# One bin to each half of TensorE's rows: the last stage of a graph layer pair with room for 320 rows a bin

## The reference, cut to what matters

```
h     = max(layernorm(x), 0)
out   = h @ W_self.T + b_self
neigh = h[dst] @ W_neigh.T + b_neigh          # one row per edge
agg   = segment_sum(neigh, src)               # rows of one source added up
count = max(segment_sum(1, src), 1)
x     = x + out + agg / count
```

## Time and profile before

| | |
|---|---|
| three runs, median (lowest to highest) | 1936.53 us (1936.05 to 1937.86) |
| the profiled execution | 1934.63 us, of which 1932.4 us is the span from the first to the last instruction |
| TensorE busy | 1740.7 us, 90% of the span, granted clock 0.955 on average |
| VectorE, ScalarE, GpSimd busy | 1463.5, 1122.0, 1138.4 us |
| the last stage, from its first matmul to its last | 1610.8 to 1922.9 us |

### The profile page before, as it was taken

How to read it: one execution, slowest core, us unless ns; L and a number is a source line. 1 busy time by engine, 2 the same in 40 slices (tenths; PEclk the granted TensorE clock), 3 DMA queues, 4 the chain that set the end, 5 groups by cost and what they waited for, 6 DMA issues and landing times. The chain is left out here.

```text
span 1932.4 us, 46473 instructions
## 1 busy us (share of the span) xinstructions
PE 1740.7 (90%) x11686; PEld 1343.8 (70%) x11686; DVE 1463.5 (76%) x4618; ACT 1122.0 (58%) x2713; POOL 1138.4 (59%) x938
## 2 busy tenths in 40 slices
PE   2659679999999999999999999999999845888998
PEld 1223257777777777777777777777777645888897
DVE  8989547877777777777777877777877625777886
ACT  1017668877777777777777777777764312333333
POOL 6970244366666666666666666666653363556676
PEclk9769769999999999999999999999999987999999
DMA  2000045677777777777777767677767556999876
GB/s 79 0 1 1 28 112 160 204 223 240 231 225 234 228 223 237 235 223 235 228 223 235 235 205 214 212 204 212 220 195 213 156 163 193 274 279 285 250 221 177
DMA packets 342167, 372.54 MB, mean 193 GB/s; under 512 B 40508, under 2 KB 269758, under 8 KB 342078
## 3 DMA queue, kind: packets, MB, share of 16 engines
q1 hardware_dynamic: 265246, 293.99, 51.2%
q0 software_dynamic: 25088, 51.83, 8.9%
q10 hardware_dynamic: 51744, 25.70, 4.4%
HBM read 251.54 MB, written 119.82 MB: 192 GB/s over the span
## 5 line engine op out<-in xcount | busy, mean ns | idle before, releaser
L764 POOL DMA_INDIRECT xg<-in_x,srcs x392 | 435.3, 1110 | 440.8 <-issue 362.0
L775 POOL DMA_INDIRECT row_table<-row_out,posq x392 | 387.3, 988 | 194.7 <-issue 125.8
L1231 PE MATMUL psum<-bin_rows,bin_hot 128*128 128x129 f32 x2352 | 288.6, 281 | 47.9 <-DVE bin_hot L1204 47.8
L1231 PEld LDWEIGHTS psum<-bin_rows,bin_hot 128*128 128x128 f32 x2352 | 274.0, 194 | 62.6 <-issue 30.8
L1102 PEld LDWEIGHTS psum<-hwin,hotT 128*128 128x128 f32 x1568 | 186.9, 195 | 78.3 <-issue 68.8
L1004 ACT ACTIVATE nhT<-psum 128x512 f32<-128x512 f32 x98 | 58.5, 597 | 309.8 <-PE psum L1074 309.8
L887 DVE TENSOR_TENSOR hotT<-dst_keys,reach 128x1024 f32<-128x1024 int32 x98 | 120.8, 1232 | 139.5 <-PE psum L1102 138.2
L1102 PE MATMUL psum<-hwin,hotT 128*128 128x128 f32 x1568 | 204.4, 285 | 15.6 <-DMA hwin<-h_table 9.9
L1091 PE MATMUL psum<-hot,win 128*128 128x128 f32 x1568 | 191.6, 275 | 1.4 <-DVE hot L859 1.4
L1091 PEld LDWEIGHTS psum<-hot,win 128*128 128x128 f32 x1568 | 183.4, 192 | 1.6 <-DVE hot L859 1.6
L1204 DVE TENSOR_TENSOR bin_hot<-iota,bin_rel 128x1536 f32<-128x1536 f32 x98 | 174.4, 1779 | 5.3
(11 more groups left out here) (174 smaller groups left out, 3761.9 us busy)
## 6 DMA issues: line engine op xcount, KB each, us to landing
win<-msg_table SPq DMA_DIRECT2D x392, 129.0 KB
hwin<-h_table SPq DMA_DIRECT2D x392, 128.0 KB
bin_rows<-row_table SPq DMA_DIRECT2D x196, 195.0 KB, 3.2
msg_table<-msgw SPq DMA_DIRECT2D x98, 258.0 KB, 4.0
nx<-in_x_nodes SPq DMA_DIRECT2D x98, 256.0 KB, 4.1
h_table<-h1s SPq DMA_DIRECT2D x98, 256.0 KB
dst_keys<-in_dst_rows SPq DMA_DIRECT2D x98, 256.0 KB
y_table<-ys SPq DMA_DIRECT2D x61, 256.0 KB, 4.1
```

What stands on the lines that cost most here:

```text
L764: nc.gpsimd.indirect_dma_start(out=xg[:, par, t, :], out_offset=None, in_=ins["x"], in_offset=bass.IndirectOffsetOnAxis(ap=srcs[:, par, t: ...
L775: nc.gpsimd.indirect_dma_start(out=row_dram, out_offset=bass.IndirectOffsetOnAxis(ap=posq[:, par, t:t + 1], axis=0), in_=row_out[:, par, t ...
L1231: last = nc.tensor.matmul(bank[2 * slot + b][:, h * MW:(h + 1) * MW], bin_hot[:, slot % 2, b, w, h * P:(h + 1) * P], bin_rows[:, slot, b, ...
```

## The change

A bin has room for 320 rows in place of 384. Its rows are laid on 64 partitions, five rows each, and the two bins of a quad lie in the two halves of the 128 partitions: bin 0 in partitions 0 to 63, bin 1 in 64 to 127. So a load moves 64 runs of 2600 bytes in place of 128 of 1560. The one-hot matrix has 5 by 256 = 1280 columns, and both halves compare with 0 to 255; a new table `qbin`, loaded at the start, holds the first node of the bin for each half. The sums become 20 matmuls over 64 rows each, with the two bins alternating: one in the lower half of the array's rows and into one bank, the next in the upper half and into the other bank. The zero rows behind the table are written by two DMAs in place of one. The limit for the general program falls to 320 with `BCAP`.

```
-BTILES = 3
-BCAP = BTILES * P
+HALF_P = P // 2
+BT = 5
+BCAP = BT * HALF_P
...
+        qbin = sb("qbin", [P, QUADS])
-        weights += [(qbase, "qbase"), (iota4, "iota4")]
+        weights += [(qbase, "qbase"), (qbin, "qbin"), (iota4, "iota4")]
...
-                sp.dma_start(row_dram[ROWS:ROWS + BCAP, :].rearrange("(p w) c -> p (w c)", p=P), pads[:, 0:BTILES * RW]).then_inc(pads_set, 16)
+                sp.dma_start(row_dram[ROWS:ROWS + 3 * HALF_P, :].rearrange("(p w) c -> p (w c)", p=HALF_P), pads[0:HALF_P, 0:3 * RW]).then_inc(pads_set, 16)
+                sp.dma_start(row_dram[ROWS + 3 * HALF_P:ROWS + BCAP, :].rearrange("(p w) c -> p (w c)", p=HALF_P), pads[0:HALF_P, 0:2 * RW]).then_inc(pads_set, 16)
...
+                def half_at(b):
+                    return slice(HALF_P * b, HALF_P * b + HALF_P)
...
-                            sp.dma_start(bin_rows[:, slot, b, :, :].rearrange("p w c -> p (w c)"),
-                                         row_dram[bass.ds(start, BCAP), :].rearrange("(p w) c -> p (w c)", p=P)).then_inc(rows_loaded[slot], 16)
+                            sp.dma_start(bin_rows[half_at(b), slot, :, :].rearrange("p w c -> p (w c)"),
+                                         row_dram[bass.ds(start, BCAP), :].rearrange("(p w) c -> p (w c)", p=HALF_P)).then_inc(rows_loaded[slot], 16)
...
-                        nc.vector.tensor_scalar(bin_rel[:], bin_rows[:, slot, :, :, C + 1], qbase[:, bass.ds(q, 1)], None, ALU.subtract).then_inc(f_rel, 1)
+                        nc.vector.tensor_scalar(bin_rel[:], bin_rows[:, slot, :, C + 1], qbin[:, bass.ds(q, 1)], None, ALU.subtract).then_inc(f_rel, 1)
...
-                        nc.vector.tensor_tensor(bin_hot[:, par, :, :, :], iota4[:].rearrange("p (b n) -> p b n", b=2).unsqueeze(2).broadcast_to([P, 2, BTILES, BIN]),
-                                                bin_rel[:].unsqueeze(3).broadcast_to([P, 2, BTILES, BIN]), ALU.is_equal).then_inc(f_hot, 1)
+                        nc.vector.tensor_tensor(bin_hot[:, par, :, :], iota4[:, 0:BIN].unsqueeze(1).broadcast_to([P, BT, BIN]),
+                                                bin_rel[:].unsqueeze(2).broadcast_to([P, BT, BIN]), ALU.is_equal).then_inc(f_hot, 1)
...
-                        for b in range(2):
-                            for h in range(2):
-                                for w in range(BTILES):
-                                    last = nc.tensor.matmul(bank[2 * slot + b][:, h * MW:(h + 1) * MW], bin_hot[:, slot % 2, b, w, h * P:(h + 1) * P],
-                                                            bin_rows[:, slot, b, w, 0:MW], start=(w == 0), stop=(w == BTILES - 1))
+                        for h in range(2):
+                            for w in range(BT):
+                                for b in range(2):
+                                    last = nc.tensor.matmul(bank[2 * slot + b][:, h * MW:(h + 1) * MW], bin_hot[half_at(b), slot % 2, w, h * P:(h + 1) * P],
+                                                            bin_rows[half_at(b), slot, w, 0:MW], start=(w == 0), stop=(w == BT - 1))
...
+        "qbin": (QROWS * np.arange(QUADS)[None] + BIN * (np.arange(P)[:, None] // HALF_P)).astype(np.float32),
```

More of the change, by code:

```diff
@@ L199, in gnn_kernel @@
         weights_loaded = sem("weights_loaded")
-        pads = sb("pads", [P, BTILES * RW])
+        pads = sb("pads", [P, 3 * RW])
         zeros_set = sem("zeros_set")
@@ L359, in _ @@
                 sp.wait_ge(starts_in, 16)
-                sp.wait_ge(pads_set, 16 * 3)
+                sp.wait_ge(pads_set, 16 * 4)
                 sp.wait_ge(weights_loaded, 16 * (len(weights) + len(rows)))
@@ L1160, in gnn_kernel @@
                 f_rc, f_mean, f_out = sf("rc"), sf("mean"), sf("out")
-                bin_rows = sems.enter_context(nc.sbuf_tensor("bin_rows", [P, 4, 2, BTILES, RW], f32))
-                bin_rel = sems.enter_context(nc.sbuf_tensor("bin_rel", [P, 2, BTILES], f32))
-                bin_hot = sems.enter_context(nc.sbuf_tensor("bin_hot", [P, 2, 2, BTILES, BIN], f32))
+                bin_rows = sems.enter_context(nc.sbuf_tensor("bin_rows", [P, 4, BT, RW], f32))
+                bin_rel = sems.enter_context(nc.sbuf_tensor("bin_rel", [P, BT], f32))
+                bin_hot = sems.enter_context(nc.sbuf_tensor("bin_hot", [P, 2, BT, BIN], f32))
                 caps = sems.enter_context(nc.sbuf_tensor("caps", [P, 2, 2], f32))
```

## The result

Four runs of the changed kernel have a median of 1925.76 us (1923.55 to 1930.65), against 1937.19 us (1936.05 to 1940.05) for the kernel before: a ratio of 0.9942 with a 95% interval from 0.992 to 0.9965, 11.4 us less. The change made the kernel faster, as forecast, but by just under half of the 23 us that the forecast had.

A forecast was written before the change was run, and what follows sets the result against it. Last stage bound late by TensorE's sums, with VectorE almost as tight, and early by bytes too; 8 us late plus 15 early is 23 off 1934.6, 1911.6, so 1913 by the runs' median; range 1895 to 2092.

The forecast's parts named there:

- The overlap: Last stage's sums on TensorE: matmuls of the two halves run side by side, 2.61 us a quad, 0.33 less; chance 0.47.
- The compare and the late regime: VectorE's compare falls 0.28 us to 1479 ns; the 37 late quads take 2.78 us for 3.00, saving 8 us.
- The early regime: First 61 quads of the last stage: 837 KB at 279 GB/s takes 3.07 us for 3.31, saving 15 us.
- the signs that the prediction gave for a wrong early term: In the early stretches: GB/s below 279 and TensorE busy over 95%.
- The start: One more table issue of 0.43 us on SP, hidden behind ScalarE's wait; nothing, or 0.5 us if uncovered.
- drain at a switch of halves: Rival in TensorE's sums: each switch between halves pauses the loads, 8.4 us a quad, some 2450 us; chance 0.04.
- The no-overlap case: Rival in TensorE's sums: each of 40 records takes its own slot, 4.72 us a quad, 2087 us; chance 0.36.
- The hidden gain: Rival: TensorE gets shorter, but held `bin_rel` and DMA wait keep the pace, 2.95 and 3.28 us, 1933; chance 0.05.
- the DMA wait: Waiting on transfers in early quads, said to keep their pace at 3.28 us in the case of a hidden gain.
- Two readings of the prediction: From TensorE's earlier trace: loads 0.31 us apart at a row-count change; a load and a matmul each last about 0.111 us.

The follow-up runs named there:

- e4: Kernel before, with y loads of quads 4 to 60 issued by ScalarE in place of SP: 1920.48 us, ratio 0.9909.
- e5: Changed kernel with y loads of quads 4 to 60 issued by ScalarE and one register load for four quads: 1892.30 us, ratio 0.9771.
- e2: Changed kernel with y loads of quads 4 to 60 issued by ScalarE in place of SP: 1904.55 us, ratio 0.9822.
- e3: Changed kernel with the eight bin starts of four quads read by one register load in place of four: 1914.07 us, ratio 0.9877.
- e7: Changed kernel with SP's y load and its wait placed behind the next quad's bin loads: 1904.51 us, ratio 0.9827.
- e9: Changed kernel with three rows per partition in place of five (64 runs of 1560 bytes), general-program limit lifted: 1888.47 us in one run.
- e10: Changed kernel with six rows per partition, so room for 384 rows as before but laid on halves: 1945.35 us, ratio 1.0044.
- e11: Kernel before, with y loads of quads 4 to 60 from ScalarE and one register load for four quads: 1918.58 us, ratio 0.9906.
- e1: Changed kernel with all ten matmuls of bin 0 before all ten of bin 1, not alternating: 2330.78 us in one run.

## Why the prediction came out as it did

*TensorE: right.* The overlap was taken as 2.61 us a quad on a slight lean, and forty loads now fit in 2.31 us with quads as near as 2.61 us (1856.87 - 1854.26). The queue does not stop at the second pass of a float32 matmul. The Trainium skill, "TensorE: Matmul & The Clock Gate", section "Part 3: Packing small matmuls", has loads for another row group pulled ahead and the matmuls run concurrently; the trace agrees, at 0.054 us a load.

*The compare and the late regime: right, a little low.* The compare takes 1.49 us (forecast 1.479), late quads 2.68 us (forecast 2.78). The bound is the one named, VectorE held by the add; the adds themselves became shorter (medians 2.16 for 2.29 us with `comb`, 1.83 for 1.93 with `xg`), which the sum left out. By the stretches the term is 0.29 x 37 = 11 us in place of 8.

*The early regime: wrong, and it is the whole shortfall.* It was to give 15 us and gave none, while the late regime gave 3 us more than forecast. The step said that a quad's 837 KB would take 3.07 us at the 279 GB/s of before, and that loads to 64 partitions should not matter, or would stay within 3.2 us a quad. The early quads took 3.34.

Two things in this step failed. The rate was no limit of the transfers: with y off SP's queue they moved 306 GB/s in the old layout (e4) and, with the register loads thinned too, 302 in the new one (e5). What set the early pace was SP's queue, its order and its length together (e2, e3, e7), for which the sum has no term. And the loads to 64 partitions did matter: each took 0.136 us more of that queue, whatever its bytes (e9), and 195 KB landed at 3.8 us for 3.2 (e10).

The two effects can be read apart. The layout alone cost some 8 us (e10). The smaller room then gave some 20 us back (1.0044 against 0.9942), 11 of them late and so some 9 early, 0.15 us a quad; the two profiles, 5 and 6.5 us above the medians of their runs, have 3.60 - 3.39 = 0.21. So what the smaller room earned early was spent by the layout in the same place. Of the signs that the prediction gave for a wrong early term, the lower rate came, and a TensorE busy over 95% did not (78 to 82%): it looked for the limit in transfers and engines, and it was in the queue.

Where SP does not bind, the change is worth 26 us (e5 against e11), near the 23 forecast. The late part of it is the forecast's own. The early part, 0.18 x 61 = 11 us, is luck and not the forecast's step: there the early quads went from TensorE's pace, 3.02 us, to 2.84, and at no rate of 279 GB/s.

*The start: right in kind.* The profiled execution of the changed kernel took 4.9 us more than its median, and its last stage began 4 us later than the one of before (1615.0 for 1610.8), while e1's and e7's, with the same table more, began at 1610.8 and 1610.2, and e4's, without it, at 1614.8. That is spread, not the table.

*The rivals.* No drain at a switch of halves: 0.054 us between loads leaves no room for one. The Trainium skill, "TensorEngine Tiling (Array Packing)", section "Key Properties", says that changing the tiling mode drains TensorE and changing the tile does not; the trace agrees with the second half of it, at 0.054 us. The no-overlap case did not come. Its price of 4.72 us a quad was worked out at the full clock; the nearest case that ran, e1, had a granted clock of 0.50 and took 7.19 us. The hidden gain came true for the early quads alone, and by SP's queue in place of the DMA wait.

Two readings of the prediction are off, with no weight for its sums. In the earlier trace rows the two loads begin 0.32 us apart, not 0.31. And the earlier trace rows show loads alone, so a load's place against a matmul cannot be read there, nor does a load last 0.111 us: its record lasts 0.186 to 0.192, and 0.111 is the step between two starts.

*Open.* What lengthens SP's register load is not settled: its median is 0.761 us in the changed kernel and 0.484 before, with single ones up to 1.5 us in both. In every kernel that reads two starts at a time, a register load that began over 2 us after SP's last DMA issue took 0.47 to 0.48 us, and the long ones all began sooner; nothing was run to tell the issue from the transfer. Nor was the longer issue itself undone by its own, since two loads with starts of their own can't be joined into one of 128 runs. So it is shown that the layout costs the early quads some 8 us, and not which part of it does: the issue time, the register load or the later landing.

## What to carry to other kernels

A stage that is paced by a queue's own instructions can look like one paced by bytes: the GB/s are steady because the issues are. Before a rate is taken as the limit of the transfers, add up the queue's issues, register loads and waits for one round, and look whether a wait stands in front of loads that do not need it. Two groups of matmuls over 64 rows, alternated, ran fully side by side here, and a change of the load's shape that comes with it must be priced on the queue that issues it and by its time to landing.

## What the runs showed of the hardware

- Alternating float32 matmuls over rows 0 to 63 and 64 to 127 ran at 0.054 us a load and matmul on average, half of the 0.111 us of full-height ones, both passes included.
- The same matmuls in an order that keeps to one half at a time ran at a granted clock of 0.50 for the stage, with TensorE busy 120.00 of 120 us (one run); 40 of them took 7.19 us, and their loads began 0.21 to 0.22 us apart except near a change of half.
- A DMA issue on SP took 0.469 us (median) for 64 runs of 1560, 2600 or 3120 bytes, and 0.333 us for 128 runs of 1560.
- In the last stage a load of 195 KB landed 3.8 us (median) after its issue when it wrote 64 partitions in runs of 3120 bytes (e10), and 3.2 us when it wrote 128 in runs of 1560 (before).
- `bin_rel`, of five or six columns, ended with GpSimd's add within 0.03 us in each pair of rows shown, and lasted 0.67 us where the shortest of before took 0.22.
